# Reordering the first stage of a four-stage layer on two engines, and writing its third stage's loop out

## What is computed

```python
x = x + local_attention(norm(x))    # each row attends to rows i-1, i, i+1; 16 heads of 16
x = x + mixture_of_experts(norm(x)) # 8 experts, top 2
x = x + delta_attention(norm(x))    # 16 heads of 64, two recurrent 64 x 64 states per head
x = x + fp4_feed_forward(norm(x))
```

```python
S = a_t * S;  S = S + b_t * kn x (v_t - kn @ S);  o = q_t @ S      # and a second state R likewise
```

## Time and profile before

| | us |
|---|---|
| median of 3 runs | 4449.84 |
| lowest and highest run | 4439.60, 4458.78 |
| the profiled execution's own time | 4420.82 |
| its span | 4418.7 |

### The profile page before, as it was taken

The page is one execution under the profiler, slowest core; times in us unless marked ns, Lnnn a source line. Parts: engine busy times, 40 slices in busy tenths (PEclk is TensorE's granted clock), DMA queues, the critical chain, the costliest instruction groups (busy, mean ns, idle before and its releaser), DMA issues. The chain is left out here.

```text
span 4418.7 us, 149376 instructions
## 1 busy us (share of the span) xinstructions
PE 3447.9 (78%) x61396; PEld 2480.5 (56%) x61396; DVE 2706.1 (61%) x5921; ACT 1433.5 (32%) x3221; POOL 949.3 (21%) x1050
## 2 busy tenths in 40 slices
PE   5644799995788878878888878888888888845777
PEld 3324566663556656656566556655665566633555
DVE  5555122222776667667766676677666767747887
ACT  1101111111344434344444344444443444421111
POOL 2225211111222221132122212221222213200000
PEclk8865899997899998889999899899988989977998
DMA  1126222222000000000000000000000000000000
GB/s 56 36 93 225 48 34 34 34 33 87 7 6 10 7 7 6 6 11 7 6 7 10 7 7 6 10 7 7 6 10 7 7 6 9 4 24 18 27 19 14
DMA packets 84359, 107.08 MB, mean 24 GB/s; under 512 B 14120, under 2 KB 74152, under 8 KB 83616
## 3 DMA queue, kind: packets, MB, share of 16 engines
q1 hardware_dynamic: 53280, 53.29, 4.0%
q0 software_dynamic: 19824, 23.03, 3.4%
q10 hardware_dynamic: 10576, 20.97, 1.3%
HBM read 59.29 MB, written 40.05 MB: 22 GB/s over the span
## 5 line engine op out<-in xcount | busy, mean ns | idle before, releaser
L993 POOL TENSOR_TENSOR da_M<-da_M,da_decay 128x512 f32<-128x512 f32 x256 | 276.9, 1113 | 756.3 <-DVE da_prev_end L1108 400.2
L1299 ACT COPY da_Ub<-da_U 32x256 f32<-32x256 f32 x1024 | 411.9, 402 | 45.1 <-ACT da_U L1292 7.3
L1133 DVE TENSOR_TENSOR da_eGn<-da_eGn,da_z 128x30 f32<-128x30 f32 (+14 forms) x960 | 352.5, 367 | 34.2 <-DVE da_z L1132 1.3
L1132 DVE TENSOR_TENSOR da_z<-da_eGn 128x30 f32<-128x30 f32 (+14 forms) x960 | 348.2, 363 | 27.6
L1580 PE MATMUL da_C<-da_Ub,da_Km 128*64 128x256 f32 x2048 | 305.7, 419 | 11.9 <-DVE da_M L1156 6.8
L1478 PE MATMUL da_unit<-da_cum,da_sp 128*128 128x132 f32 x1024 | 216.6, 386 | 116.5 <-DVE da_ssm L1087 80.7
L1412 PE MATMUL da_unit<-da_wx,da_xnT 128*128 128x512 f32 x512 | 253.8, 620 | 24.0 <-ACT da_xnT L1245 22.1
L766 PE MATMUL moe_ps_up<-moe_up,moe_zsT 128*128 x568 | 270.1, 598 | 1.4 <-ACT moe_zsT L685 1.4
L1478 PEld LDWEIGHTS da_unit<-da_cum,da_sp 128*128 128x128 f32 x1024 | 193.4, 283 | 128.8 <-issue 121.3
L1419 PE MATMUL da_unit<-da_xnT,da_wx 128*128 128x128 f32 x2048 | 256.3, 286 | 11.1 <-ACT da_eGn L1284 9.6
L1419 PEld LDWEIGHTS da_unit<-da_xnT,da_wx 128*128 128x128 f32 x2048 | 248.4, 202 | 20.0 <-issue 15.2
(11 more groups left out here) (291 smaller groups left out, 7304.5 us busy)
## 6 DMA issues: line engine op xcount, KB each, us to landing
moe_zs<-moe_slots SPq DMA_DIRECT2D x71, 129.0 KB, 2.0
moe_up<-in_upT ACTq DMA_DIRECT2D x8, 1024.0 KB, 13.8
moe_down<-in_downT ACTq DMA_DIRECT2D x8, 1024.0 KB, 12.8
la_x<-in_x SPq DMA_DIRECT2D x16, 256.0 KB, 3.4
stream<-la_y SPq DMA_DIRECT2D x32, 128.0 KB, 2.1
moe_x<-stream SPq DMA_DIRECT2D x8, 512.0 KB, 5.4
da_x<-moe_acc SPq DMA_DIRECT2D x128, 32.0 KB, 1.9
stream<-da_xz SPq DMA_DIRECT2D x128, 32.0 KB, 1.5
```

Source lines behind the costliest of these rows:

```text
L993: ins = nc.gpsimd.tensor_tensor(st_, st_, decay[:, par, rec, 2 * g:2 * g + 2].rearrange("p a b -> p (a b)").unsqueeze(2).to_broadcast([P, ...
L1132: c.link(tt(t, Xm[:, s + 1:C, s:s + 1].to_broadcast([P, below, s]), Xm[:, s:s + 1, 0:s].to_broadcast([P, below, s]), ALU.mult))
L1133: c.link(tt(Xm[:, s + 1:C, 0:s], Xm[:, s + 1:C, 0:s], t, ALU.add))
L1299: ins = nc.scalar.copy(Ub[rows_of(b), :, :, b, :], U[rows_of(b), rec])
```

## The change

It has two parts. In the local attention ACT's order within a step becomes `turned_out(s-2)`, `exps(s-1)`, `normalised(s+3)`, `turned(s+2)`, and PE's becomes `products(s+1, 0)`, `turned_out(s-2)`, `products(s+1, 1)`, `projected(s-2)`, `turned(s+2)`. No instruction is added or removed and no buffer changes. In the delta attention the hardware loop goes: all 33 periods are written out one after the other on each engine, every wait has a constant, and the trip registers, their arithmetic and the branch disappear.

```diff
             for s in STEPS:                      # ACT
                 if here(s - 2):
                     turned_out(s - 2)
-                if here(s + 2):
-                    turned(s + 2)
                 if here(s - 1):
                     exps(s - 1)
                 if here(s + 3):
                     normalised(s + 3)
+                if here(s + 2):
+                    turned(s + 2)
...
             for s in STEPS:                      # PE
+                if here(s + 1):
+                    products(s + 1, 0)
                 if here(s - 2):
                     turned_out(s - 2)
                 if here(s + 1):
-                    products(s + 1, 0)
+                    products(s + 1, 1)
                 if here(s - 2):
                     projected(s - 2)
-                if here(s + 1):
-                    products(s + 1, 1)
                 if here(s + 2):
                     turned(s + 2)
...
         def need(eng, sem, at):
-            if not isinstance(at, int):
-                wait_apart(eng, sem, at)
-            elif at > 0:
+            if at > 0:
                 eng.wait_ge(sem, at)
-        def every_period(eng, period, enter=None, leave=None):
-            period(-1, 1)
-            period(0, 0)
-            with eng.Fori(0, TRIPS) as k:
-                if enter is not None:
-                    enter(k)
-                for u in range(UN):
-                    period(k * UN + (FIRST + u), 1 - u % 2)
-                if leave is not None:
-                    leave()
-            for i in range(FIRST + UN * TRIPS, NCH):
+        def every_period(period):
+            for i in range(-1, NCH):
                 period(i, i % 2)
```

More of the change, by code:

```diff
@@ L896, in delta_attention @@
         once = lambda i, g: i * NG + (g + 1)
-        chunk_rows = lambda a, i, b: a[bass.ds(i * C + b * S, C), :] if not isinstance(i, int) else a[i * C + b * S:i * C + b * S + C, :]
+        chunk_rows = lambda a, i, b: a[i * C + b * S:i * C + b * S + C, :]
         LOADS = 17
-        FIRST, LAST_FULL = 1, NCH - 3
-        UN = 4
-        TRIPS = (LAST_FULL - FIRST) // UN
         def need(eng, sem, at):
-            if not isinstance(at, int):
-                wait_apart(eng, sem, at)
-            elif at > 0:
+            if at > 0:
                 eng.wait_ge(sem, at)
-        def every_period(eng, period, enter=None, leave=None):
-            period(-1, 1)
-            period(0, 0)
-            with eng.Fori(0, TRIPS) as k:
-                if enter is not None:
-                    enter(k)
-                for u in range(UN):
-                    period(k * UN + (FIRST + u), 1 - u % 2)
-                if leave is not None:
-                    leave()
-            for i in range(FIRST + UN * TRIPS, NCH):
+        def every_period(period):
+            for i in range(-1, NCH):
                 period(i, i % 2)
         def exists(n):
-            return not isinstance(n, int) or n < NCH
+            return n < NCH
         def flags(i):
-            if not isinstance(i, int):
-                return True, True, True, True
             return i >= 0, i + 1 < NCH, i + 2 < NCH, i >= 1
@@ L960, in period @@
                     residual(i + 2)
-                    if not isinstance(i, int) or i + 3 < NCH:
+                    if i + 3 < NCH:
                         load_x(i + 3)
@@ L965, in _ @@
             load_x(1)
-            every_period(sp_, period)
+            every_period(period)
             need(sp_, added, 16 * B * NCH)
@@ L1036, in _ @@
             norms(0)
-            every_period(pool, period, lambda k: pc.enter(k, 2 * UN), lambda: pc.leave(TRIPS))
+            every_period(period)
             put_out(NCH - 1)
@@ L1237, in _ @@
                 add_bias(0, u)
-            PER_TRIP = UN * (4 + 1 + 2 + 3 + 3 + 2 * (C - 2) + 1 + NG * 3)
-            every_period(dve, period, lambda k: c.enter(k, PER_TRIP), lambda: c.leave(TRIPS))
+            every_period(period)
         @block.scalar
@@ L1386, in _ @@
             rate_log(0)
-            every_period(act, period)
+            every_period(period)
             turned_outputs(NCH - 1, 3)
@@ L1729, in _ @@
                 rates(0, 0, u)
-            every_period(pe, period)
+            every_period(period)
             turned_outputs(NCH - 1, 3)
```

## The result

The changed kernel takes 4262.6 us (median of 4 runs, 4260.6 to 4269.8) against 4452.5 us: ratio 0.958, 95% interval 0.9555 to 0.9605. Timed once more with five runs it took 4242.6 us, ratio 0.9565 (0.9546 to 0.9584). The forecast was 4240 us in a range of 4195 to 4305.

A forecast was written before the change was run, and what follows sets the result against it. It took one-engine-at-a-time steps to bound the local attention and loop instructions and jumps to lengthen delta attention's periods. Gains of 62 and 148 us, 210 together, off the median 4449.8 gave 4240 us, range 4195 to 4305.

The forecast's parts named there:

- The ring in the local attention: Local attention: only one engine works at a time in the 17.07 us step; reordering makes it 11.6, gaining 62 us.
- PE's way round: Local attention: PE's loop of first eviction 1.0, block without turned input 9.9, signal and result 0.7: 11.6 us a step.
- the edges: Local attention: edge DMAs, 13.4 us long, no longer hidden; DVE waits 1.8 us in three places, 5.4 us lost.
- The collision of POOL and DVE: Local attention: POOL's residual sums lie beside DVE's weighing and cost DVE 0.5 us a step, making its work 11.5.
- The copy behind the norm: Local attention: ACT's copy `turned(s+2)` now stands behind `normalised(s+3)`, costing nothing while a step is over 10.6 us.
- Period 29: Delta attention: the period already written out, 82.2 us against 88.5 looped, taken as a sample of the changed code.
- The correction by the clock: Delta attention: 0.5 us per hundredth of granted clock, so 82.2 at 0.94 becomes 83.7 at 0.91; 83.2 was taken.
- the rival that called period 29 a lucky one: Delta attention: written-out periods stay near 86.5 us, gain 56 there, total 4330 to 4370 us; chance 0.10.
- The jumps: Delta attention: six jumps back of the loop, at most 5 us each, 1 us per period.
- the rival that kept PE at its lower clock: Local attention: PE stays at 1.2 GHz, gain 24 us there plus 148 in delta attention, 4278 us; chance 0.07.
- the 24 us of the range's small end: Local attention: the smallest gain allowed for, with PE kept at 1.2 GHz; with 98 in delta attention it gives 4328 us.
- The slower and the no-change rival: Whole kernel: denser PE stream in delta attention granted less clock, chance 0.03; time stays within 0.5%, 22 us, chance 0.02.

## Why the prediction was right

- **The ring in the local attention** was read rightly: ACT's copy tied DVE to PE's block. Forecast 62 us, measured 64 (300.1 to 235.9). The step was sized at 11.6 us and is 11.8, and part of that closeness is luck: the 11.6 came from PE's way round, which isn't the bound. PE's block is 8.3 us in that step, turned input included (147.22 to 155.51), where the forecast had 9.9 without it, and PE waits; DVE's own work is what fills the step. And the step, 0.2 us longer than forecast, is made up for by the edges, which cost less.
- **The collision of POOL and DVE** was foreseen in kind and missed in place. The residual sums run beside DVE's weighing and cost it nothing (L262 takes 1.83 us as before). But being slow themselves (2.13 us for 1.40) they delay POOL's neighbours' sums, and those run beside L246: 2.90 instead of 2.01 us. The 0.5 us I put in was 0.9. Neither engine lost the other's whole length: L192 took 1.87 us beside it, where it takes 1.27 alone. Moving the residual away gave back 0.88 a step there and cost 0.45 at L218, 0.44 in all.
- **The edges** do make every fourth step wait, with 1.6 to 1.7 us as forecast (1.8). The step itself grows by 0.55 only, some 2 us in all where 5.4 were put in, since L246 then starts after POOL's sum has ended and is short (1.83 us at 77.66, after 1.66 us of waiting).
- **The copy behind the norm** costs nothing, as I had it: PE's first products wait for the eviction (2.32 us ahead of 147.22).
- **The delta attention** was the mis-sized term: 148 us forecast, 123 measured. The step that failed is to take one written-out period as a sample of all: "Period 29 took 82.2 at 0.94", and from it 83.2 for each. The straight periods average 84.4 us over six profiles, and single ones range from 80.4 to 88.5. The correction by the clock doesn't hold either: in the changed kernel's first profile periods at a granted clock of 0.94 took 80.4, 85.3 and 84.9 us, and those from 0.88 to 0.98 differ by some 2.7 us, half of the 0.5 us per hundredth. So the rival that called period 29 a lucky one was right in part, with 84.4 between my 83.2 and its 86.5. Period 29 was 82.1 to 82.6 in four of the five profiles with four periods a trip, and in straight kernels it is 83.0 to 86.9; why it is short behind the loop, no run shows. The measured 123 us lie halfway between the forecast and its small end (28 x 3.5 = 98 us).
- **The jumps** were priced at up to 5 us each by the wait ahead of L1478; they cost 3 to 5, depending on how one measures.
- **The clock** rose a little in the delta attention, 0.90 or 0.91 to 0.92, and much in the local attention's steps, 0.80 to 0.93, with the shorter idle time. So the rival that kept PE at its lower clock fell; its sign, products of 4.9 us for both tiles, did not show: the second tile's take 2.75 us. No view gives this clock in GHz. In the kernel before, the granted clock is 0.50 from 172.0 to 178.5 us and 1.00 from 179.0 to 189.0, and its mean over the step 0.80. Nor does a run show the 24 us of the range's small end: PE's order alone gained 20.5 us (300.1 to 279.6), ACT's alone 63.1, both together 64. The slower and the no-change rival have nothing left.
- **The sum**: 64 + 123 = 187 us, against 190 and 191 in the two timings. The first pair of profiles differs by 160 only, as that of before had quick periods and that of the change a first expert matmul that came 11 us later. The forecast's 210 was 25 too much in one term and 2 too little in the other.

## What to carry to other kernels

When one engine's in-order stream holds a short instruction that has long been ready behind one that closes another engine's block, look for the ring that this makes: the order on the least busy engine can set the step (ACT's order alone took it from 17.07 us to 11.8 to 12.1). Here the instructions that a loop's waits needed cost more in total than its jumps (some 52 us against 19 to 30), so judge a hardware loop by whole periods inside and outside of it, but by many: one period outside is one draw from a spread of several per cent (80.4 to 88.5 us). And after a stage is shortened, look at its transfers that were hidden before: a DMA over 127 rows was free at a step of 17 us and held up every fourth step at 11.8 and 11.4.

## What the runs showed of the hardware

- A DMA between rows of SBUF with 127 rows moved 254 KB at 26 GB/s or less, at 0.07 of the 16 DMA engines' time. Cut into 112 and 15 rows it moved at up to 261 GB/s, at 0.97 of their time, and the 112 rows landed 2.5 us after issue.
- In the kernel before step after step takes 17.07 us, each with slow first products (4.87 us, after 6.54 us of idle time) and fast second ones (2.74 us), and a granted clock of 0.80. In the kernel with PE's order alone the steps alternate between 15.9 us (first products 5.33 us, clock 0.81) and 14.8 us (4.21 us, clock 0.86), with the same 5.41 us of idle time ahead of each.
- DVE's TENSOR_SCALAR on two columns took 0.62 us beside POOL's residual sums, and 0.17 us without them.
- From the local attention's end to the first expert matmul the same code takes 169 or 170 us in some profiles and 175 to 181 in others: up to 11 us that no edit explains, as much as some of the effects looked for here.
